# Turning the FFN input of a fused attention and FFN kernel: from transposes on TensorE to a quadrant-exchanged load and 32x32 transposes on VectorE

## The reference, cut to what matters

```
x = layernorm(x + attn(x))        # attn: pre-norm, q/k/v, causal softmax, o_proj, residual
x = layernorm(x + ffn(x))
def ffn(x):                       # x is the 8192 x 512 output of the first line, "x1" in the kernel
    p = softmax(x @ wr.T)         # 8 experts
    top 2 of p, renormalised: gates
    h = silu(x @ w1.T); h = silu(h @ w3.T); h = h @ w2.T
    out = zeros_like(x); out[indices_k] += gates_k * h     # rows 0 to 7 of out alone are written
```

## Time and profile before

| | |
|---|---|
| time, median of 3 runs | 1724.53 us (1723.97 to 1726.92) |
| span of the profiled execution | 1729.0 us |
| PE busy in it | 1697.6 us, 98% |
| DVE, ACT, POOL busy | 46%, 39%, 16% |
| loads of `x1_in` | 16 of 1 MB, 5.5 us (SP) and 7.8 us (ACT) from issue to landing, medians |

### The profile page before, as it was taken

How to read it: one execution, slowest core, us unless ns; L and a number is a source line. 1 busy time by engine, 2 the same in 40 slices (tenths; PEclk the granted TensorE clock), 3 DMA queues, 4 the chain that set the end, 5 groups by cost and what they waited for, 6 DMA issues and landing times.

```text
span 1729.0 us, 23965 instructions
## 1 busy us (share of the span) xinstructions
PE 1697.6 (98%) x8179; PEld 1400.9 (81%) x8179; DVE 788.8 (46%) x2104; ACT 670.0 (39%) x1301; POOL 282.0 (16%) x491
## 2 busy tenths in 40 slices
PE   7999999999999999999999999999999999999998
PEld 5888888878888887888888888888878888888886
DVE  5454433455353454445344554534444443444443
ACT  4443333343342344334224433423344444444442
POOL 1220201121120111112011211201122121212111
PEclk9999999999999999999999999999999999999999
DMA  4111201121110112121111222112230101010100
GB/s 152 56 49 50 68 31 37 62 82 60 56 68 31 37 60 70 61 68 55 43 37 49 73 68 68 49 40 72 87 103 25 49 24 49 24 49 24 49 0 7
DMA packets 50116, 92.58 MB, mean 54 GB/s; under 512 B 5456, under 2 KB 5456, under 8 KB 50016
## 3 DMA queue, kind: packets, MB, share of 16 engines
q1 hardware_dynamic: 38064, 70.31, 11.8%
q10 hardware_dynamic: 11952, 20.99, 3.9%
HBM read 57.71 MB, written 33.57 MB: 53 GB/s over the span
## 4 chain that ended last, share of the span: by engine, by line
PE 82%; issue 12%; POOL 2%; ACT 2%; DVE 1%; DMA 1%; POOLq 0%; SPq 0%; ACTq 0%; DVEq 0%
PE psum L330 24%; PE psum L332 24%; PE psum L331 24%; PE psum L1186 3%; PE psum L1278 1%; PE psum L1124 1%; PE psum L1288 1%; PE psum L1296 1%; PE psum L1295 1%; PE psum L1287 1%; POOL expo L510 1%; POOL rstd L435 1%; ACT xin L561 1%; DMA raw<-in_wk_t 1%; ACT affine L545 0%
## 5 line engine op out<-in xcount | busy, mean ns | idle before, releaser
L330 PE MATMUL psum<-xt_hi,g_hi 128*128 128x512 f32 (+3 forms) x640 | 242.4, 379 | 0.4 <-DVE g_lo L834 0.4
L332 PE MATMUL psum<-xt_lo,g_hi 128*128 128x512 f32 (+3 forms) x640 | 232.0, 362 | 0.0
L331 PE MATMUL psum<-xt_hi,g_lo 128*128 128x512 f32 (+3 forms) x640 | 230.8, 361 | 0.0
L609 ACT ACTIVATE pt_hi<-psum 128x512 fp32r<-128x512 f32 (+3 forms) x160 | 84.8, 531 | 373.3 <-PE psum L1186 366.0
L330 PE MATMUL psum<-v_hi,pt_hi 128*128 128x512 f32 x544 | 223.0, 410 | 1.6 <-DVE pt_lo L844 1.1
L332 PE MATMUL psum<-v_lo,pt_hi 128*128 128x512 f32 x544 | 213.3, 392 | 0.0
L331 PE MATMUL psum<-v_hi,pt_lo 128*128 128x512 f32 x544 | 212.7, 391 | 0.0
L432 POOL TENSOR_TENSOR var_eps<-meanvar,eps 128x2 f32<-128x2 f32 (+1 forms) x97 | 19.3, 199 | 1070.2 <-DVE meanvar L812 1065.7
L849 DVE TENSOR_REDUCE rowmax<-psum 128x1 f32<-128x512 f32 (+3 forms) x160 | 97.7, 611 | 201.7 <-PE psum L332 200.9
L731 ACT ACTIVATE act_f<-psum 128x512 f32<-128x512 f32 x128 | 76.6, 598 | 241.4 <-PE psum L332 241.4
L510 POOL TENSOR_TENSOR expo<-euler,shifted 128x32 f32<-128x32 f32 x16 | 87.3, 5455 | 325.1 <-DVE shifted L1036 325.1
(11 more groups left out here) (146 smaller groups left out, 3379.6 us busy)
## 6 DMA issues: line engine op xcount, KB each, us to landing
xin<-in_x ACTq DMA_DIRECT2D x64, 256.0 KB, 2.8
tok<-in_x SPq DMA_DIRECT2D x64, 256.0 KB, 2.6
x_scratch<-tok SPq DMA_DIRECT2D x64, 256.0 KB, 2.1
out_dram<-tok SPq DMA_DIRECT2D x64, 256.0 KB, 2.0
x_in<-x_scratch SPq DMA_DIRECT2D x14, 1024.0 KB, 5.5
xin<-in_w_t ACTq DMA_DIRECT2D x8, 256.0 KB, 2.8
x_in<-x_scratch ACTq DMA_DIRECT2D x2, 1024.0 KB, 7.8
w_sb<-in_w_t SPq DMA_DIRECT2D x1, 1024.0 KB, 5.7
```

The source lines that it names most:

```text
L330: pe.matmul(o, ws, ms, start=first, stop=False, skip_group_check=True)
L331: pe.matmul(o, w_lo, ms, start=False, stop=False, skip_group_check=True)
L332: return pe.matmul(o, ws, m_lo_, start=False, stop=last, skip_group_check=True)
L609: act.activation(pt_hi[:, n % 2, 0:w], psum[:, turn_bank(turn_use(t, c)), 0:w], ACT.Copy).then_inc(pt_hi_ready, 1)
```

## The change

The load is cut by quadrants of 32 partitions: `x1_in[q*32 + j, slot, c, t*32 + i]` gets x1 of row t*32 + j and feature c*128 + q*32 + i. That is 4 DMAs for a load, each of 2048 runs of 32 floats, 128 bytes. Then each 32 x 32 block only has to be transposed within its quadrant, which DVE does with one instruction for a chunk of 128 x 512, from SBUF to SBUF (`x1t_f`). PE's 16 transposes of a group, and its waits on the loads and on the banks, are taken out. ACT and DVE read `x1t_f` in SBUF where they read PSUM. DVE turns the next group's four chunks after the gates and ahead of `split_x1(0)`; the first group's are turned in `split_first_x1`, which now stands ahead of the last tile's `residual`. DVE's loop is written out for two groups, since the slot alternates. `x1t_f` takes the place of `h1_hi` and `h1_lo`, which move behind `not_yet_free`.

```diff
-        x1_in = sb("x1_in", [P, 2, GROUP, D], F32, stage2)
+        x1_in = sb("x1_in", [P, 2, DC, GROUP * P], F32, stage2)
...
+        x1t_f = sb("x1t_f", [P, DC, GROUP * P], F32, stage2)
...
+        QUADRANTS, LANES = 4, 32
+        LOADS = QUADRANTS * DMA
+        def load_x1(engine, slot, first_row):
+            rows_of = x1_scratch[bass.ds(first_row, GROUP * P), :].rearrange("(t j) (c q i) -> q j c t i", j=LANES, q=QUADRANTS, i=LANES)
+            for q in range(QUADRANTS):
+                engine.dma_start(x1_in[q * LANES:(q + 1) * LANES, slot].rearrange("j c (t i) -> j c t i", i=LANES),
+                                 rows_of[q]).then_inc(x1_loaded[slot], DMA)
...
@@ SP, and in the same way ACT's first two loads
-                    sp.dma_start(x1_in[:, s], x1_scratch[bass.ds((2 * h + s) * 512, 512), :].rearrange("(t p) d -> p t d", p=P)).then_inc(x1_loaded[s], DMA)
+                    load_x1(sp, s, (2 * h + s) * (GROUP * P))
...
@@ ACT
-            def turn_x1(i, c):
+            def round_x1(i, c):
                 act.wait_ge(x1_turned, i * DC + c + 1)
-                act.activation(x1t_hi[:, c, :], psum[:, c, :], ACT.Copy).then_inc(x1t_hi_ready, 1)
+                act.activation(x1t_hi[:, c, :], x1t_f[:, c, :], ACT.Copy).then_inc(x1t_hi_ready, 1)
...
@@ DVE, last attention tile
+                    split_first_x1()
                     residual(b, TILES - 1)
-                    split_first_x1()
                     norm_behind(b, TILES - 1)
...
+            def turn_x1(slot, c):
+                dve.transpose(x1t_f[:, c, :], x1_in[:, slot, c, :]).then_inc(x1_turned, 1)
             def split_first_x1():
+                dve.wait_ge(x1_loaded[0], LOADS)
+                for c in range(DC):
+                    turn_x1(0, c)
                 for c in range(DC):
                     dve.wait_ge(x1t_hi_ready, c + 1)
-                    dve.tensor_tensor(x1t_lo[:, c, :], psum[:, c, :], x1t_hi[:, c, :], ALU.subtract).then_inc(x1t_ready, 1)
+                    dve.tensor_tensor(x1t_lo[:, c, :], x1t_f[:, c, :], x1t_hi[:, c, :], ALU.subtract).then_inc(x1t_ready, 1)
...
@@ DVE, group, after the gates
                 if not last:
+                    dve.wait_ge(x1_loaded[1 - parity], loads)
+                    dve.wait_ge(x1t_ready, i * DC + DC)
+                    for c in range(DC):
+                        turn_x1(1 - parity, c)
                     split_x1(0)
                     split_x1(1)
...
@@ PE, group
-                if not last_group:
-                    pe.wait_ge(x1_loaded[1 - parity], loads(parity))
-                    for c in range(2):
-                        pe.wait_ge(h1_hi_ready, 1 + i * 4 + c + 1)
-                        turn_x1(1 - parity, c)
...
-                    if n == 2 and not last_group:
-                        pe.wait_ge(x1t_ready, (i + 1) * DC + 2)
...
-                    if n == 2 and not last_group:
-                        for c in (2, 3):
-                            pe.wait_ge(h2_hi_ready, 1 + i * 4 + c - 1)
-                            turn_x1(1 - parity, c)
...
@@ PE, ahead of the first group
-            pe.wait_ge(x1_loaded[0], DMA)
             pe.wait_ge(probs_ready, 1 + B * CHUNKS)
-            for c in range(DC):
-                turn_x1(0, c)
```

More of the change, by code:

```diff
@@ L225, in attention_mlp @@
         whole.enter_context(stage2)
-        x1_in = sb("x1_in", [P, 2, GROUP, D], F32, stage2)
+        x1_in = sb("x1_in", [P, 2, DC, GROUP * P], F32, stage2)
         x1t_hi = sb("x1t_hi", [P, DC, GROUP * P], F32R, stage2)
         x1t_lo = sb("x1t_lo", [P, DC, GROUP * P], F32R, stage2)
-        h1_hi = sb("h1_hi", [P, DC, GROUP * P], F32R, stage2)
-        h1_lo = sb("h1_lo", [P, DC, GROUP * P], F32R, stage2)
+        x1t_f = sb("x1t_f", [P, DC, GROUP * P], F32, stage2)
         wr_s = sb("wr_s", [P, DC, P], F32R, stage2)
@@ L236, in attention_mlp @@
         wr_raw = sb("wr_raw", [P, DC, E], F32, stage2)
-        taken = 2 * GROUP * D + 4 * DC * GROUP * P + DC * P + GROUP * P + 4 * D + DC * E
+        taken = 2 * GROUP * D + 3 * DC * GROUP * P + DC * P + GROUP * P + 4 * D + DC * E
         sb("not_yet_free", [P, 2 * DC * S - taken + (1 + SLOTS) * D + 64], F32, stage2)
+        h1_hi = sb("h1_hi", [P, DC, GROUP * P], F32R, stage2)
+        h1_lo = sb("h1_lo", [P, DC, GROUP * P], F32R, stage2)
         act_f = sb("act_f", [P, 2, D], F32, stage2)
@@ L690, in tile @@
                     for i in range(2):
-                        act.dma_start(x1_in[:, i], x1_scratch[i * 512:(i + 1) * 512, :].rearrange("(t p) d -> p t d", p=P)).then_inc(x1_loaded[i], DMA)
+                        load_x1(act, i, i * GROUP * P)
                     act.dma_start(wr_raw[:], wr_t.rearrange("(c p) n -> p c n", p=P)).then_inc(wr_loaded, DMA)
@@ L743, in group @@
                 if not last:
-                    turn_x1(i + 1, 0)
-                    turn_x1(i + 1, 1)
+                    round_x1(i + 1, 0)
+                    round_x1(i + 1, 1)
                 for n in range(GROUP):
                     if n == 3 and not last:
-                        turn_x1(i + 1, 2)
-                        turn_x1(i + 1, 3)
+                        round_x1(i + 1, 2)
+                        round_x1(i + 1, 3)
                     act.wait_ge(h2_product, i * 4 + n + 1)
@@ L758, in _ @@
             for c in range(DC):
-                turn_x1(0, c)
+                round_x1(0, c)
             norm_behind(B - 1, TILES - 1)
@@ L1002, in _, with group @@
             ROUTE = 15
-            def group(i, last):
+            def group(i, last, parity, loads):
                 count = [0]
@@ L1074, in group @@
                     split_h2(n)
-            with dve.Fori(0, NG - 1) as i:
-                group(i, False)
+            with dve.Fori(0, NG // 2 - 1) as h:
+                group(2 * h, False, 0, h * LOADS + LOADS)
+                group(2 * h + 1, False, 1, h * LOADS + 2 * LOADS)
+            group(NG - 2, False, 0, NG // 2 * LOADS)
             at_batch[0], count[0] = B - 1, last_own[0]
             norm_behind(B, 0, 1, 2)
-            group(NG - 1, True)
+            group(NG - 1, True, 1, 0)
             dve.wait_ge(rows_loaded, DMA)
@@ L1273, in _ @@
             batch(B - 1, True)
[L1276 to L1279, removed]
             def gate(i, n, before=False):
@@ L1288, in gate, with group @@
                 pe.matmul(psum[:, ACC, :], gates_s[:, n, :], h2_lo[:, n % 2, :], start=False, stop=False, skip_group_check=True).then_inc(gated, 1)
-            def group(i, last_group, parity):
+            def group(i):
                 pe.wait_ge(logits_copied, 1 + i)
@@ L1348, in _ @@
                 for parity in range(2):
[L1349 to L1357, removed]
+                    group(2 * h + parity)
+            group(NG - 2)
+            group(NG - 1)
             gate(NG - 1, 3)
```

## The result

The changed kernel takes 1761.59 us (median of 4 runs, 1758.38 to 1763.02) against 1724.37 us of the kernel before in the same comparison: 2.0% slower, ratio 1.0201 (95% interval 1.0189 to 1.0214), +37 us. The forecast had the sign and a third of the size, and its range ended at 1760.

The account below looks back on a forecast made before the run. PE, busy 98% of the span, was taken to bound the kernel. -24.3 for transposes removed plus 15 x (1.95 + 0.11) gave +6.6, and +7.1 for the head made +13.7: 1738 us, range 1722 to 1760.

Parts of the forecast that it names:

- turns off PE, 15 groups: Stage 2: without PE's transposes a group takes 26.45 us, 1.62 less; 15 groups save 24.3 us.
- the gate's wait, net with the line above: Stage 2, `gate(i, 0)`: ready 1.95 us late behind DVE's transposes and splits; groups of 28.51 us, +6.6 over 15.
- head: Before stage 2's first h1: the first two loads delay `wr_raw` to 1268.7, so h1 starts at 1274.5, +7.1 us.
- The rival at the cast's 0.43: Gate: transposes take 0.43, ACT's path binds, groups of 27.55 us; total 1720 to 1724, chance 0.19.
- ACT's six more issues at some 0.5 us end at about 1249.3: Head: ACT's added load issues end just ahead of its next work at 1249.61, so they were costed at nothing.
- issues that grow with the number of runs: Head, part of the rival of much later first loads: ACT held to 1259; time 1749 to 1775, chance 0.13.
- The step that I put in the sum instead: Head: `wr_raw` queued behind the first loads at 19 ns a run lands at 1268.7 and delays DVE; +7.1 us.
- my line: Load price: line through 15 ns for 32-byte and 97 ns for 2 KB runs, giving 19 ns at 128 bytes.
- A landing before 1260: Head: sign of a wrong forecast; `wr_raw` landing before 1260 would take 8 us off the sum.
- the prediction's case in which `wr_raw` lands in time: Head: h1 then waits for POOL's `fold_ready` and eight router matmuls and starts at 1266.2, -1.2 us.
- full granted clock: PE in the kernel before: busy 98% of the span at full granted clock throughout; no clock term in the sum.
- The loads in the loop: Stage 2: a load takes 9.7 us plus its start, landing about 12 us after issue, hidden two groups ahead.

Follow-up runs that it names:

- both edits: The changed kernel with the first two loads issued by SP and the four DVE transposes moved ahead of h1 splits: 1699.6 us, ratio 0.9840.
- loads alone: The kernel before with only the new 128-byte-run loads, TensorE still turning the input: 1742.25 us, ratio 1.0087.
- work in the wait: The changed kernel with eight more matmuls of unused product on PE just ahead of each group's first gate: 1748.0 us, ratio 1.0117.

## Why the prediction was right in sign and wrong in size

| term | forecast | measured |
|---|---|---|
| turns off PE, 15 groups | -24.3 | -25 (28.07 to 26.38 a group, both edits) |
| the gate's wait, net with the line above | +6.6 | +6.3 in the trace |
| head | +7.1, by a late `wr_raw` | +12.5 in the trace, +15.9 timed (loads alone), by ACT |
| clock after the gate's wait | none | +12 in the trace, 14 to 16 timed (work in the wait) |

- **The gate: right.** Transposes of 0.67 us, four in 2.49 (forecast 0.68 and 2.48), a wait of 1.78 to 1.95 (1.95), groups without a fall of 28.5 (28.51). The rival at the cast's 0.43 is out. The Trainium skill's one element per cycle per lane (Vector Engine (DVE) Microarchitecture Reference, section 3.8, The reshape front-end and per-opcode configuration) agrees with that: 0.67 us is the pace of the 0.68 rows.
- **The head: the first failed step.** "ACT's six more issues at some 0.5 us end at about 1249.3" stood among the edits that cost nothing. With `wr_raw` they ended at 1257.3, and PE waited 12.2 us in the last attention tile. The case was named among the rivals, as issues that grow with the number of runs, 14.7 us to 1259, at a chance of 0.13; the eight took 14.3. That the number fits is partly luck, since half as many runs did not halve the issues. The step that I put in the sum instead was wrong twice over. A run cost some 14 ns on a full queue (an estimate: 1.8 us for 128 runs, if the 2048 of a DMA are spread evenly over 16 engines), not 19; my line joined two unlike prices, 97 ns of the packets' own time and 15 ns of time on the clock. And `wr_raw` landed at 1259.8, before DVE needed it. A landing before 1260 was the sign that I had named against this term; it came, but the head did not get shorter, because ACT held PE first. With the loads on SP and `wr_raw` ahead of them the head is -1.0 us, near the -1.2 of the prediction's case in which `wr_raw` lands in time.
- **The clock: the second failed step, a term left out.** I carried full granted clock over from a kernel in which PE hardly waits to one that waits 1.8 to 1.95 us in each group. The gap from +13.7 to +37.2 is 23.5 us, and the clock behind the gates is 12 to 16 of it. The lower clock in the head, some 2.4 us, was not in the sum either.
- **The loads in the loop: right.** They are hidden: inner groups of 28.06 us with them alone. In the changed kernel a load lands 9.2 to 10.2 us after its first issue (forecast about 12), and with four DMAs of 2 KB runs 6.7 to 7.0. The Trainium skill's request for transfers of 512 bytes or more for line rate (DMA: Bandwidth & Descriptors, Specifications) agrees in direction with these times.

## What to carry to other kernels

Work that leaves the bound engine must not come back as a wait of it: look for a place in the new engine's own list where it waits for something else, and put the moved work there; here that turned +37 us into -12, and with the first loads issued by SP into -27. Price a wait of TensorE with the clock that may follow it, and try it by filling the wait with matmuls that do nothing. Count the runs of a DMA where it is issued as well as where it lands, and let an engine issue it behind which nothing waits.

## What the runs showed that I had not expected

- A wait of 1.8 to 1.95 us in each group, with PE otherwise full, brings the clock to its lower level in 8 to 10 of 15 groups, at 1.5 us each; waits of 1.2 to 1.3 and of 0.6 to 0.7 us bring none in 15.
- Eight DMAs of 256 KB each hold the engine that issues them for 14 us with 128-byte runs, ACT and SP alike, and for 4 us with 2 KB runs, while half as many runs, of 256 bytes, shorten an issue on the busy queue by only a tenth and the eight together by a quarter, to 10.7 us.
- 128 useless matmuls made the kernel 14 to 16 us faster.
